# Attention and mixture-of-experts block on one core: a second buffer for the block-moved probabilities, and ScalarE issuing half of the moves

## What is computed

```python
logits = jnp.einsum('bqhd,bkhd->bhqk', q, k) / jnp.sqrt(q.shape[-1])
logits = jnp.where(mask, logits, neg)            # causal
probs = jax.nn.softmax(logits, axis=-1)
out = jnp.einsum('bhqk,bkhd->bqhd', probs, v)
...
x = x + ga * attn(h)
h = layernorm(x) * (1 + cb) + sb
logits = xf @ Wr.T + br
expert_idx = jnp.argmax(logits, axis=-1)
h = relu(einsum('td,efd->etf', xf, W1) + b1); y = einsum('etf,edf->etd', h, W2) + b2
```

## Time and profile before

| | |
|---|---|
| runs without profiler, median of 2 | 1029.34 us (1029.2 to 1029.48) |
| the profiled execution | 1032.4 us |
| its span (first to last instruction) | 1030.6 us |
| granted TensorE clock, mean over the span | 0.965 of full speed |
| TensorE (PE) busy | 89% of the span |
| VectorE (DVE) busy | 74% |
| ScalarE (ACT) busy | 61% |
| GpSimd (POOL) busy | 11% |

### The profile page before, as it was taken

One profiled execution on the slowest core, in us unless ns is written; L12 is line 12 of the kernel. 1 busy time (PEld: TensorE's weight loads), 2 busy tenths in 40 slices (PEclk: granted clock), 3 DMA queues, 4 the chain that ended last, 5 costly groups with the idle time before them and its releaser, 6 DMA issues.

```text
span 1030.6 us, 18821 instructions
## 1 busy us (share of the span) xinstructions
PE 919.4 (89%) x6147; PEld 681.8 (66%) x6147; DVE 758.8 (74%) x2400; ACT 626.7 (61%) x1159; POOL 110.2 (11%) x125
## 2 busy tenths in 40 slices
PE   3999989898998989998989899998999899868797
PEld 2676657675676757675767667675766566546697
DVE  4898748794797848894879578875898389774454
ACT  2876548574685648665757468564875466542375
POOL 0200001000100010000200010001000011101244
PEclk9999989999999999999999999999999899988899
DMA  3005430353014520543036302551053201356020
GB/s 77 11 22 132 106 72 14 90 135 84 21 48 112 120 50 12 127 110 84 14 73 148 87 21 53 127 113 36 23 118 87 66 6 46 95 155 174 25 64 26
DMA packets 154306, 76.91 MB, mean 75 GB/s; under 512 B 20647, under 2 KB 151507, under 8 KB 154210
## 3 DMA queue, kind: packets, MB, share of 16 engines
q1 hardware_dynamic: 152962, 73.58, 29.7%
q0 software_dynamic: 1248, 2.13, 0.7%
HBM read 18.21 MB, written 11.77 MB: 29 GB/s over the span
## 4 chain that ended last, share of the span: by engine, by line
PE 38%; SPq 27%; DVE 17%; DMA 8%; issue 6%; ACT 3%; another core or an unknown queue 1%; POOLq 0%; POOL 0%; DVEq 0%; ACTq 0%
SPq L667 24%; PE ps L910 11%; DMA turned_far<-staged 7%; PE ps L874 6%; PE ps L885 6%; DVE staged L1269 6%; PE ps L853 4%; DVE probs L1254 4%; PE ps L857 3%; PE ps L1034 2%; PE ps L1045 2%; DVE probs L1257 2%; SPq L686 1%; SPq L697 1%; ACT probs L1099 1%
## 5 line engine op out<-in xcount | busy, mean ns | idle before, releaser
L1099 ACT ACTIVATE probs<-probs,neg_max 128x128 f32<-128x128 f32 (+15 forms) x256 | 308.9, 1207 | 150.2 <-DVE neg_max L1261 147.3
L874 PE MATMUL ps<-k_both,q_both 128*128 128x512 f32 (+2 forms) x1280 | 358.8, 397 | 9.0 <-DVE probs L1254 2.8
L1254 DVE TENSOR_SCALAR_CACHE_REDUCE probs<-ps 128x512 f32<-128x512 f32 (+1 forms) x384 | 245.5, 666 | 22.5 <-PE ps L885 10.8
L874 PEld LDWEIGHTS ps<-k_both,q_both 128*128 128x128 f32 x1280 | 203.7, 189 | 78.7 <-issue 28.7
L1107 ACT COPY pT<-ps 128x512 f32<-128x512 f32 (+1 forms) x342 | 178.1, 549 | 113.5 <-PE ps L885 104.8
L885 PE MATMUL ps<-ident,probs 128*128 128x128 f32 x1472 | 213.1, 274 | 1.4 <-ACT probs L1099 0.5
L885 PEld LDWEIGHTS ps<-ident,probs 128*128 128x128 f32 x1472 | 174.8, 141 | 42.3 <-issue 15.4
L910 PE MATMUL ps<-pT,v_sb 128*64 128x256 f32 (+1 forms) x1600 | 174.3, 366 | 9.9 <-DVE oT L1305 7.5
L910 PE MATMUL ps<-turned_far,v_sb 128*64 128x256 f32 x704 | 104.1, 454 | 58.7 <-DMA turned_far<-staged 58.7
L910 PEld LDWEIGHTS ps<-pT,v_sb 128*64 128x64 f32 x1600 | 108.2, 137 | 72.8 <-issue 12.4
L1257 DVE CUSTOM_DVE_ANT_0 probs<-ps,causal 128x256 f32<-128x256 f32 (+3 forms) x256 | 130.6, 510 | 26.4 <-PE ps L874 26.1
(11 more groups left out here) (145 smaller groups left out, 680.5 us busy)
## 6 DMA issues: line engine op xcount, KB each, us to landing
turned_far<-staged SPq DMA_DIRECT2D x384, 96.0 KB
x_sorted<-blank SPq DMA_DIRECT2D x19, 458.5 KB, 5.2
rinv_b<-spread_rows SPq DMA_DIRECT2D x128, 64.0 KB, 2.7
turned_far<-staged SPq DMA_DIRECT2D x128, 64.0 KB
spread_rows<-rinv_rows SPq DMA_DIRECT2D x256, 0.5 KB
probs<-in_L_ffn_W_dram SPq DMA_DIRECT2D x1, 2048.0 KB, 9.5
w_pair<-in_L_attn_w_qkv_dram SPq DMA_DIRECT2D x24, 64.0 KB, 2.1
hT<-x_sorted SPq DMA_DIRECT2D x23, 65.5 KB
```

Of the source, the lines that this page charges most:

```text
L874: m = pe.matmul(ps_ring[:, s.bank, 0:w], q_split[r % 2][:, q0:q0 + P], k_split[r % 2][:, part, k0:k0 + w], start=(part == 0), stop=(part = ...
L1099: act.activation(row, row, ACT.Exp, bias=neg_max[:, g, r:r + 1], accum_out=row_sum[:, g, r:r + 1]).then_inc(exp_done, 1)
L1254: dve.tensor_scalar(row, ps_ring[:, bank, 0:w], 1.0, LOWEST, ALU.mult, ALU.max, accum_out=highest).then_inc(bank_free[bank], 1)
```

## The change

- `turned_far` gets two buffers (`FAR_BUFS` = 2); a move waits for the far PVs of the move *before the last*, and moves signal two semaphores by turns.
- Of the 16 DMAs of a move SyncE issues 8 ("move", a = 0, 1), ScalarE the other 8, as a new kind "push" (a = 2, 3) in ScalarE's list and in `FIRST`. The helper `move_blocks` issues four DMAs on either queue, with the waits ahead of them. The planner takes `PUSH` = 1000 ns for a push, and `ISSUE` 650 for 430.
- Groups 5 to 7 have 5 far tiles, where there were 6; group 4 keeps 4. So 24 tiles more are turned on TensorE and taken (3 a pair), and the same number fewer are shuffled and moved.
- `pT` has 5 slots where there were 8. Planner constants: `PV_BATCH` 8 to 3, `SCORE_LEAD` 1.4 to 1.1, `SCORE_TILES` 18 to 24, `TAKE_ACT` 0 to -1500, `TAKE_DVE` 2500 to 1500, `ADD_DVE` 0 to 1000, `PROJ_LEAD` 2 to 2.5.
- The small tables of the experts' part lie in `staged` and no longer in `pT`.

```diff
-PT_SLOTS = 8
-STAGED = 6
-FAR = {4: 4, 5: 6, 6: 6, 7: 6}
-ISSUE = 430.0
+PT_SLOTS = 5
+STAGED = 5
+FAR = {4: 4, 5: 5, 6: 5, 7: 5}
+FAR_BUFS = 2
+ISSUE = 650.0
 LAND = 4000.0
+PUSH = 1000.0
-PV_BATCH = 8
+PV_BATCH = 3
...
+        keys["push"] = [(p, g, a) for p, g in self.moves for a in (2, 3)]
...
-    FIRST = dict(act=("hi", "value"), dve=("sum", "norm", "lo"))
+    FIRST = dict(act=("hi", "value", "push"), dve=("sum", "norm", "lo"))
...
             begin = max(self.at("shuffle", p, g, r) for r in range(4))
+            if m >= FAR_BUFS:
+                q, f = self.moves[m - FAR_BUFS]
+                begin = max(begin, self.at("pv", q, f, far(f) - 1))
             if m:
-                q, f = self.moves[m - 1]
-                begin = max(begin, self.at("pv", q, f, far(f) - 1), self.move_at(m - 1)[0] + 16 * ISSUE)
+                begin = max(begin, self.move_at(m - 1)[0] + 8 * ISSUE)
...
-            self.moved[m] = begin + HOP, begin + HOP + 16 * ISSUE + LAND
+            self.moved[m] = begin + HOP, begin + 2 * PUSH + HOP + 8 * ISSUE + LAND
...
-        turned_far = sb("turned_far", [P, STAGED, P // SQUARE, 4 * SQUARE])
+        turned_far = sb("turned_far", [P, FAR_BUFS, STAGED, P // SQUARE, 4 * SQUARE])
...
+        def move_blocks(queue, key):
+
+            p, g, a = key
+            m = plan.move_no[p, g]
+            queue.wait_ge(shuffled, 4 * m + 4)
+            if m >= FAR_BUFS:
+                q, f = plan.moves[m - FAR_BUFS]
+                queue.wait_ge(pv_done, plan.order[q, f, far(f) - 1] + 1)
+            for b in range(P // SQUARE):
+                queue.dma_start(turned_far[b * SQUARE:(b + 1) * SQUARE, m % FAR_BUFS, 0:far(g), a, :],
+                                staged[a * SQUARE:(a + 1) * SQUARE, 0:far(g), b, :]).then_inc(moved[m % 2], 16)
...
+                elif s.kind == "push":
+                    move_blocks(act, s.key)
...
-                        dve.wait_ge(moved, 256 * m)
+                        dve.wait_ge(moved[(m - 1) % 2], 256 * ((m - 1) // 2) + 256)
```

More of the change, by code:

```diff
@@ L21 @@
 CHUNKS = 4
-PT_SLOTS = 8
-STAGED = 6
-FAR = {4: 4, 5: 6, 6: 6, 7: 6}
-ISSUE = 430.0
-LAND = 4000.0
-PV_BATCH = 8
[L28 to L33, removed]
+PT_SLOTS = 5
[3 more added lines that the diff above has]
+ISSUE = 650.0
+LAND = 4000.0
+PUSH = 1000.0
+PV_BATCH = 3
+SCORE_LEAD = 1.1
+SCORE_TILES = 24.0
+TAKE_ACT = -1500.0
+TAKE_DVE = 1500.0
+ADD_DVE = 1000.0
+PROJ_LEAD = 2.5
 NE = 8
@@ L189, in ready @@
             return max(self.turned_at(key), at("value", p, key[2] // 4), free)
+        if kind == "push":
+            return self.move_at(self.move_no[p, g])[0]
         if kind == "shuffle":
@@ L286, in transfers @@
         for m, (p, g) in enumerate(self.moves):
-            for a in range(4):
+            for a in range(2):
                 steps.append((self.move_at(m)[0] + 4 * ISSUE * a, "move", (p, g, a)))
@@ L329, in took @@
             return far(key[1]) * P / 0.96 + 100.0
+        if kind == "push":
+            return PUSH
         if kind == "top":
@@ L508, in adaln_block @@
         blank = sb("blank", [P, ROW])
-        turned_all = pT[:].rearrange("p s c -> p (s c)")
-        hidT = turned_all[:, 0:4 * FF].rearrange("p (s f n) -> p s f n", s=4, f=FT)
-        table_end = [4 * FF]
+        hidT = pT[:, 0:4, :].rearrange("p s (f n) -> p s f n", f=FT)
+        staged_all = staged[:].rearrange("p j b c -> p (j b c)")
+        table_end = [0]
         def table(n, width):
@@ L517, in table @@
             table_end[0] = first + n * width
-            return turned_all[:, first:first + n * width].rearrange("p (r c) -> p r c", c=width)
+            return staged_all[:, first:first + n * width].rearrange("p (r c) -> p r c", c=width)
         PAD_E = NE // 2
@@ L585, in adaln_block @@
         shuffled = sem("shuffled")
-        moved = sem("moved")
+        moved = [sem(f"moved{i}") for i in range(2)]
         pv_done = sem("pv_done")
@@ L658, in _ @@
                 if s.kind == "move":
[L659 to L664, removed]
-                        sp.wait_ge(pv_done, plan.order[q, f, far(f) - 1] + 1)
-                    for b in range(P // SQUARE):
-                        sp.dma_start(turned_far[b * SQUARE:(b + 1) * SQUARE, 0:far(g), a, :],
-                                     staged[a * SQUARE:(a + 1) * SQUARE, 0:far(g), b, :]).then_inc(moved, 16)
+                    move_blocks(sp, s.key)
                 elif s.kind == "w1":
@@ L716, in _ @@
                                  blank[:].unsqueeze(1).broadcast_to([P, end - first, ROW])).then_inc(blanked, 16)
-            sp.wait_ge(moved, 256 * len(plan.moves))
+            for i in range(2):
+                sp.wait_ge(moved[i], 256 * len(range(i, len(plan.moves), 2)))
             sp.wait_ge(chosen_known, 1)
@@ L902, in _ @@
                         if j == 0:
[L903 to L904 removed]
+                            pe.wait_ge(moved[plan.move_no[p, g] % 2], 256 * (plan.move_no[p, g] // 2) + 256)
+                        of_head = turned_far[:, plan.move_no[p, g] % FAR_BUFS, j, :, :].rearrange("p a (u h i) -> p h u a i", u=2, h=2)
                     else:
```

4 lines of the change are left out of this document (1 added, 3 removed).

## The result

The changed kernel takes 1052.8 us (1051.15 and 1054.44), before 1029.34 us: a ratio of 1.0228 with a 95% interval of 1.0159 to 1.0297. It is slower; whether by more than 2% the interval leaves open. I forecast 999 us with 975 to 1032. The forecast has the wrong sign.

The account below looks back on a forecast made before the run. TensorE's work plus its idle time, mainly waits for moves, was taken as the bound. 1030.6 - 54 - 10 + 9.5 + 10.6 + 10 + 4 = 1000.7 us of span, so 999 us measured, with a range of 975 to 1032.

Parts of the forecast that it names:

- What bounds the kernel, and why moves are long: TensorE, 89% busy, bounds the kernel; far PVs wait 58.7 us for moves, whose 16 issues on SyncE take 11.24 us.
- my 54 us: TensorE's waits ahead of far PVs: shorter moves remove all but 5 of 58.7 us, a gain of 54 us.
- rival B: SyncE's and ScalarE's queues cannot issue together, so moves stay long and ScalarE is held: 1081 us, chance 0.08.
- ScalarE's issues: + 10 us: Eight issues of 0.65 us hold up ScalarE's takes and exponentials; a tenth of 102 us reaches the time, + 10 us.
- The sequencer decodes on during compute work: ScalarE's DMA issues would overlap compute instructions ahead of them, putting their term nearer 0 than 10 us.
- Clock: - 10 us: TensorE's matmuls after long waits: six of seven such waits go, each saving 1.7 us of lower-clock running, - 10 us.
- Turned tiles and alternations, + 9.5 and + 10.6 us: On TensorE, 24 more turned tiles cost 9.5 us; 84 more PV entries, less fewer kind changes, cost net 10.6 us.
- VectorE: + 4 us: TensorE sometimes finds no score bank free because VectorE is busy: half a us a pair, + 4 us.
- A: ScalarE becomes the second bound, its issues occupying it wholly and delaying TensorE: 1022 us as middle, chance 0.16.
- C: Small buffers: five slots and batches of three make TensorE wait for takes, 12 us in all: 1011 us, chance 0.10.
- D's floor: Floor case in which ScalarE and VectorE add nothing: 985 us, chance 0.06.

## Why the prediction was wrong, point by point

- **What bounds the kernel, and why moves are long.** Right. Issuing is the cost; with two queues a move is short enough, and the far waits fell from 58.7 us to none (my 54 us). The second buffer gives nothing, as said.
- **The queues issue together (against rival B).** Right: 5.23 and 5.54 us side by side. The Trainium skill's rule of a generator block that is shared and locked for each issue (Perfetto Trace Analysis, "DMA Instruction — HWDGE (DVE, Sync)") does not show here as a longer issue: medians of 0.63 and 0.62 us with both queues, 0.61 us with SyncE alone.
- **ScalarE's issues: + 10 us.** This is the step that failed: "Most of it is caught by these; I take a tenth, 10 us. Bounds: 0, and 42 us if 1.3 us of each block show." Against the kernel without a block (977 us) the term is 75 us (85 us up to the last far PVs). The upper bound that I worked out first was 102 us, 3.2 us of excess for each of 32 blocks; 2.4 us of each came through, near a third of it as slower matmuls behind the waits, which the term did not have at all. I then cut it to a tenth because TensorE had waited for a take only once. But that row belongs to another order, planned with eight slots and without issues on ScalarE. The new one was planned for 2 us of a block that lasts 5.2, and at that price its takes come too late; told 2.6 us for four issues, the planner wins back 41 us. Which property of the new order makes it so sensitive is not shown: the batches of three by themselves are not it, since with eight the waits for takes grew (from 62.1 to 78.2 us).
- **The sequencer decodes on during compute work.** By the Trainium skill (Perfetto Trace Analysis, "DVE / Act Engine Instruction") the sequencer is free for the next instruction once it has pushed a compute instruction into its queue. The trace agrees, but it helps little here: the issues at 594.99 start while the copies from 594.49 still run, about 0.6 us of overlap for a block of 6.7, and 19 us of 184 over the whole program. A block has only one or two copies ahead of it to lie over. With single issues between the compute instructions it was 130 of 168 us. For blocks of eight it does not carry the term to 0, as I let it stand.
- **Clock: - 10 us.** Wrong in the changed kernel (0.970), since the new wait in group 7 took the old one's place: 3.80 us and a clock of 0.60 behind it. Where that wait is 0.78 us the clock is 0.982, and TensorE's busy time 929.3 us.
- **Turned tiles and alternations, + 9.5 and + 10.6 us.** Together with the clock I forecast + 10.1 us of busy time; with four issues it is 929.3 - 919.4 = + 9.9 us, with one buffer + 6.1, with GpSimd and the same lists + 4.1. The sum is right or somewhat too high; its parts no run shows one by one.
- **VectorE: + 4 us.** Not found: no wait of TensorE for a score that VectorE has yet to copy appears with the changed kernel's lists and four issues, or with GpSimd. Its own busy time grew by 6.3 us (my 5).
- **The rivals.** A came nearest: waits of TensorE for takes above 30 us, its sign, came true with 62. But its reason, a ScalarE wholly occupied, did not: with its issues counted ScalarE is busy for some 76% of the span and not over 85 (630.7 + 184 - 19 us of 1049.4). A gave 1022 us, at most 1031, with a chance of 0.16; its 1015 for half the price is a slip, 1000.7 - 10 + 21 - 1.3 makes 1010. Of the chance of a slower kernel, 0.10, 0.07 hung on B, which was the wrong mechanism. Rival B's general sentence, that the change turns into a loss once a block costs TensorE over 1.3 us a move, is what happened, with 2.4 us. C is out for batches of three: with the same slots and lists, and no block, TensorE waits for takes for 1.0 us. And that kernel's 977 us lies below D's floor of 985: the other terms together, 1000.7 - 10 - 1.3 = 989 us, were 12 us too high.

## What to carry to other kernels

Moving DMA issues to a compute engine takes that engine away for their whole length (here 0.63 us each) in one piece, and what counts is not its busy share (60%, some 76% with the issues) but how soon someone needs what stands behind the piece: up to the last far PVs, four in a row cost 7 to 12 us against none on ScalarE (898.3 and 903.1 us for 891.3), eight cost 85 us. When an order is planned from assumed durations, its slack is as small as those say, so look at what the plan assumes of a new step and take the excess over that in full as your upper end. Give such issues to an engine that nobody waits for, if there is one, or keep the pieces short. GpSimd was such an engine in the pairs, but not in the closing steps, where 8 us were lost again. Single issues between compute instructions were mostly hidden, but they drew the move out, and that kernel took 1017 us.

## What was not expected of the hardware

- GpSimd issues such a DMA in 0.573 us (median), less than SyncE (0.612) and ScalarE (0.628 in the changed kernel), and VectorE is not slower for it: it is busy for 764.7 us, 765.1 in the changed kernel. The kernel takes 977 us with 256 of them.
- Waits for takes of up to 2.1 us left TensorE's granted clock at 0.986 with six issues; with single waits of up to 3.7 and 3.8 us it was 0.971 and 0.970. Between six and eight issues 19 us of busy time hang on it, beside the waits themselves. The mean over the span is a rough guide, though: the kernel with GpSimd and new lists shows 0.975 with TensorE busy for only 927.0 us, and there it is 0.99 up to 870 us and 0.82 behind.
- The best kernels are those with four DMAs on ScalarE, 973 us with one buffer and 975 with two, which cannot be told apart; over 5% below the kernel before. There TensorE is 95% busy, and what it still waits for lies mostly in the start and in the closing steps.
